# A four-layer network on one core: accumulating scatters, channel mixing in another order, token mixing rewritten

## The reference

```
x = layernorm(x + block_sparse_attention(x))
# mixture of experts 1: E = 8, hidden 512, every token to its 2 best experts, no capacity
probs = softmax(x @ Wg); topv, topi = top_k(probs, 2); topv /= sum(topv)
moe   = sum over the 2 experts of topv * (gelu(x @ Wu[e]) @ Wd[e]);  shared = gelu(x @ W1) @ W2
x = layernorm(x + shared + moe)
# token mixing (a recurrence over the sequence; rms(x) = x * rsqrt(mean(x*x) + 1e-6)), channel mixing
x_in = x; n = rms(x); k, v, r = n @ Wk.T, n @ Wv.T, sigmoid(n @ Wr.T)
state' = ew * state + k*v;  wkv = state + eu * k*v
x = x + mixer_scale * (r * wkv @ Wo.T)
h = leaky_relu(rms(x) @ Wfc.T, 0.5);  x = x + mlp_scale * (h * h @ Wmlp.T)
x = layernorm(x_in + x)          # x_in is what the block was given, x its output
# mixture of experts 2: E = 8, hidden 1024, capacity 640 rows per expert, weights softmax(top 2)
x = layernorm(x + sum over the 2 experts of weight * ((silu(x @ W1[e]) * (x @ W2[e])) @ W3[e]))
```

## Time and profile before

| | us |
|---|---|
| median of 3 runs (2108.09 to 2112.3) | 2112.03 |
| the profiled execution's own time | 2117.18 |
| its span, first to last instruction | 2115.4 |
| PE busy (matmul) | 1739.3 (82%) |
| PE busy (weight load) | 1390.0 (66%) |
| DVE busy | 1202.9 (57%) |
| ACT busy | 881.9 (42%) |
| POOL busy | 599.5 (28%) |
| mean granted TensorE clock | 0.889 of full |

### The profile page before, as it was taken

One profiled execution on the slowest core, in us unless ns is written; L12 is line 12 of the kernel. 1 busy time (PEld: TensorE's weight loads), 2 busy tenths in 40 slices (PEclk: granted clock), 3 DMA queues, 4 the chain that ended last, 5 costly groups with the idle time before them and its releaser, 6 DMA issues. The chain is left out here.

```text
span 2115.4 us, 36910 instructions
## 1 busy us (share of the span) xinstructions
PE 1739.3 (82%) x12492; PEld 1390.0 (66%) x12493; DVE 1202.9 (57%) x2736; ACT 881.9 (42%) x1739; POOL 599.5 (28%) x765
## 2 busy tenths in 40 slices
PE   5759999999994798699999387758887399999970
PEld 4625766666672477577887144457886399999970
DVE  4557677777733766333332488546664655555546
ACT  3200666666682264332232144433442044444336
POOL 1330011111113387423222644122221122312114
PEclk9955899999996599899999699979998599999995
DMA  5694233333303561122222421050001333322206
GB/s 200 245 145 56 53 78 73 76 73 77 75 13 103 172 229 70 50 64 71 64 62 62 142 69 56 0 202 21 21 11 63 100 106 123 108 84 72 77 9 238
DMA packets 142011, 191.00 MB, mean 90 GB/s; under 512 B 70465, under 2 KB 105123, under 8 KB 140864
## 3 DMA queue, kind: packets, MB, share of 16 engines
q1 hardware_dynamic: 113280, 131.79, 20.2%
q0 software_dynamic: 20992, 51.80, 9.0%
q10 hardware_dynamic: 7616, 5.77, 1.5%
HBM read 125.98 MB, written 65.54 MB: 91 GB/s over the span
## 5 line engine op out<-in xcount | busy, mean ns | idle before, releaser
L583 DVE TENSOR_REDUCE att_neg_max<-att_m_ps 128x1 f32<-128x320 f32 x496 | 234.7, 487 | 129.9 <-PE att_m_ps L410 122.3
L410 PE MATMUL att_m_ps<-att_k,att_q 96*128 96x384 f32 x496 | 229.3, 474 | 28.4 <-DMA att_k<-qk 21.0
L1827 PE MATMUL silu_h_ps<-silu_xT,silu_w_part 128*128 128x320 f32 x1536 | 237.9, 312 | 6.4 <-DVE silu_h L1935 3.2
L1827 PEld LDWEIGHTS silu_h_ps<-silu_xT,silu_w_part 128*128 128x128 f32 x1536 | 227.7, 189 | 9.4 <-issue 4.1
L410 PEld LDWEIGHTS att_m_ps<-att_k,att_q 96*128 96x128 f32 x496 | 103.6, 209 | 137.3 <-DVE att_neg_max L583 87.6
L1612 PE MATMUL gelu_y_ps<-layer_wd,gelu_hT 128*128 x576 | 138.0, 382 | 7.8 <-issue 7.1
L548 ACT ACTIVATE att_prob_f<-att_b_ps 128x1024 f32<-128x1024 f32 x64 | 65.6, 1024 | 172.6 <-PE att_b_ps L434 172.6
L2380 PE MATMUL mlp_y_ps<-mlp_wm_part,mlp_h_part 128*128 128x256 f32 x768 | 108.9, 311 | 28.2 <-DVE mlp_h_part L2491 28.2
L2380 PEld LDWEIGHTS mlp_y_ps<-mlp_wm_part,mlp_h_part 128*128 128x128 f32 x768 | 107.3, 220 | 30.4 <-DVE mlp_h_part L2491 30.4
L1573 POOL DMA_INDIRECT gelu_x<-rows,gelu_row_no x72 | 71.7, 996 | 173.7 <-PE gelu_x_ps L1584 156.5
L1612 PEld LDWEIGHTS gelu_y_ps<-layer_wd,gelu_hT 128*128 128x128 f32 x576 | 103.8, 190 | 23.3 <-issue 12.0
(11 more groups left out here) (313 smaller groups left out, 3825.3 us busy)
## 6 DMA issues: line engine op xcount, KB each, us to landing
experts_w<-in_dram SPq DMA_DIRECT2D x24, 1024.0 KB
qk<-qkv_part POOLq DMA_DIRECT2D x32, 512.0 KB, 3.3
att_k<-qk SPq DMA_DIRECT2D x192, 64.0 KB, 2.3
att_q<-qk SPq DMA_DIRECT2D x168, 64.0 KB, 3.0
expert_rows<-gelu_y SPq DMA_DIRECT2D x72, 128.0 KB, 1.7
expert_rows<-mlp_zero SPq DMA_DIRECT2D x8, 1024.0 KB, 16.5
v<-qkv_v POOLq DMA_DIRECT2D x8, 544.0 KB, 4.8
att_v<-v SPq DMA_DIRECT2D x8, 544.0 KB, 4.2
```

The source lines that it names most:

```text
L410: nc.tensor.matmul(bank[:, 0:2 * LOCAL].rearrange("p (a n) -> p a n", a=2), q[b][0:MROW, x, :], local_and_global(b, x), start=True, stop=T ...
L583: ins = nc.vector.tensor_reduce(neg_max[p % 2][:, x:x + 1], m_ps[u % 2][:, 0:LOCAL + 2 * BLK], AX.X, ALU.max, negate=True)
L1827: mm = nc.tensor.matmul(h_ps[u % 2][a][:, :], w12_part[f % RING][wp][:, a, k, :], xT[s][xp][:, k, rows], start=(i == 0), stop=(i == 3 * KD ...
```

## The change

It has five parts.

1. *First experts.* DVE multiplies y by `share`, a weight for each row of each tile, when it takes it from PSUM, and POOL adds the tile to `part` (which holds x + shared) with an accumulating indirect DMA. Each waits for the landing of the one before. The gather of tile n + 6 stands ahead of the scatter of tile n in POOL's queue; y gets four buffers. Empty rows have number T and are skipped. The second experts do the same into `summed`, with five buffers.
2. *Routing.* The one-hot product gives four columns instead of one or two: the token's number and the two halves (high, rest) of its weight, for either choice; `in_tile` gets three columns for each choice. From it come `table` (both forms of the row number) and `share`.
3. *Token mixing.* It reads `part` alone; no gathers and no weighted sums. Both norms' roots come from one variance, the first scaling (n1) moves to ACT, the second rms scaling goes: since leaky relu and square turn a scaling of a row into its square, the factor `share` (one over the mean square) is put on in channel mixing's last addition. The order on all engines is new, with products, turns and projections dealt among one another; base has three buffers.
4. *Channel mixing.* The downs of group g - 1 stand between the ups of group g, after slices 2, 4, 5 and 7, and the turn of group g - 2 before the last slice; `h_part` has two buffers, `out` is written over x. The normed rows are stored twice, to `rows` and to `summed` (the start value of the second experts' sum). No zeros are written.
5. *End and loops.* `combine` becomes `last_norm`: it loads `summed` (4 MB) and does the layer norm, statistics on DVE, scaling on ACT. All hardware loops over groups, tiles and experts are written out.

```diff
@@ experts_gelu
-        @block.sync
-        def _(sp):
-            with sp.Fori(0, NT // 2) as i:
-                for s in range(2):
-                    n = 2 * i + s
-                    sp.wait_ge(y_ready, n + 1)
-                    sp.dma_start(y_d[bass.ds(n * P, P), :], y[s][:, :]).then_inc(y_out[s], 16)
...
+            def gather(n):
+                s = n % XS
+                if n >= XS:
+                    pool.wait_ge(x_turned, n - XS + 1)
+                nc.gpsimd.indirect_dma_start(out=x[s][:, :], out_offset=None, in_=x_d,
+                                             in_offset=bass.IndirectOffsetOnAxis(ap=table[:, 1, n:n + 1], axis=0)
+                                             ).then_inc(x_in[s], 16)
+
+            for n in range(XS + 2):
+                gather(n)
+            for n in range(NT):
+                if n + XS + 2 < NT:
+                    gather(n + XS + 2)
+                pool.wait_ge(y_ready, n + 1)
+                if n > 0:
+                    pool.wait_ge(y_out, 16 * n)
+                nc.gpsimd.indirect_dma_start(out=sum_d, out_offset=bass.IndirectOffsetOnAxis(ap=table[:, 0, n:n + 1], axis=0),
+                                             in_=y[n % YS][:, :], in_offset=None, bounds_check=T - 1, oob_is_err=False,
+                                             compute_op=ALU.add).then_inc(y_out, 16)
...
-                dve.wait_ge(y_out[s], 16 * (n // 2))
-                nc.vector.tensor_copy(y[s][:, :], y_ps[s][:, :]).then_inc(y_ready, 1)
+                if n >= YS:
+                    dve.wait_ge(y_out, 16 * (n - YS + 1))
+                nc.vector.tensor_scalar(y[n % YS][:, :], y_ps[s][:, :], share[:, n:n + 1], None, ALU.mult).then_inc(y_ready, 1)
@@ route
+            settle(nc.vector.tensor_copy(halves[:, :, :], weight[:, :, :]))
+            for a in range(2):
+                nc.vector.tensor_copy(entry[:, :, a, 2 * a], tokens[:, :])
+                nc.vector.tensor_copy(entry[:, :, a, 1 - a], halves[:, a, :].bitcast(F32))
+                settle(nc.vector.tensor_tensor(entry[:, :, a, 2 - a], weight[:, a, :], halves[:, a, :].bitcast(F32), ALU.subtract))
...
-                nc.vector.tensor_tensor(in_tile[half % HALVES][:, :, :, :], in_tile[half % HALVES][:, :, :, :].bitcast(F32),
-                                        tokens[:, bass.ds(N * q, N)].rearrange("p (t a b) -> p t a b", a=1, b=1).broadcast_to(tiled),
+                spread = [P, 2 * N, COLS - 1, NT]
+                nc.vector.tensor_tensor(in_tile[half % HALVES][:, :, :, :, :].rearrange("p t a c n -> p (t a) c n"),
+                                        is_tile[half % HALVES][:, :, :, :].rearrange("p t (a b) n -> p (t a) b n", b=1).broadcast_to(spread),
+                                        entry[:, N * q:N * (q + 1), :, :].rearrange("p t a (c b) -> p (t a) c b", b=1).broadcast_to(spread),
                                         ALU.mult).then_inc(made, 1)
@@ mix_tokens, VectorE's step (all of it is new)
+            def step(g):
+                if exists(g + 2):
+                    stats(g + 2)
+                if exists(g + 1):
+                    scan(g + 1, 0)
+                if exists(g + 2):
+                    inverses(g + 2)
+                if exists(g):
+                    add(g, (0,))
+                if exists(g + 1):
+                    weigh(g + 1, 0)
...
+                if exists(g):
+                    add(g, (2, 3))
+                if exists(g + 2):
+                    normalised(g + 2)
+                if exists(g + 1):
+                    scan(g + 1, 1)
+                    weigh(g + 1, 1)
+                    gated(g + 1, 1)
+                if exists(g - 1):
+                    shares(g - 1)
@@ mix_channels, TensorE
-            def step(g, s):
-                if exists(g):
-                    for f in range(1, KF):
-                        up(g, s, f)
-                if exists(g + 1):
-
-                    up(g + 1, 1 - s, 0)
-                if exists(g - 2):
-                    norm.turn(pe, g - 2, s)
-                if exists(g):
-                    down(g, s)
-
-            skewed(pe, -1, 2, step, start=4)
+            for g in range(NGRP + 3):
+                for f in range(KF):
+                    if exists(g):
+                        up(g, f)
+                    if exists(g - 1) and f in AFTER:
+                        down(g - 1, AFTER.index(f))
+                    if exists(g - 2) and f == KF - 2:
+                        norm.turn(pe, g - 2, g % 2)
@@ mix_channels, VectorE's addition
-                    nc.vector.tensor_tensor(out[s][:, j, :], y_ps[j % 2][:, :],
-                                            x[:, bass.ds(g * GT + j, 1), :].rearrange("p a d -> p (a d)"),
-                                            ALU.add).then_inc(summed, 1)
+                nc.vector.scalar_tensor_tensor(out[g][:, j, :], y_ps[j % 2][:, :], share[:, t:t + 1], x[:, t, :],
+                                               ALU.mult, ALU.add).then_inc(summed, 1)
```

1017 lines of the change are left out of this document (449 added, 568 removed).

## The result

The changed kernel takes **2062.2 us** (median of four runs, 2058.7 to 2067.6) beside 2112.2 for the kernel before on the same chip: a ratio of 0.977, 95% interval 0.974 to 0.979. The forecast was 2027, its range 1996 to 2080. So the sign and the range held, and the gain is 50 us where the sum said 85.

The account below looks back on a forecast made before the run. No single engine bounds the program; gaps lie in the stages rewritten. Terms 0 + 7 + 6 - 49 - 31 - 18 = -85 take the profiled 2117.2 us to 2032, 2027 as median; range 1996 to 2080.

Parts of the forecast that it names:

- the first experts' scatter: First experts: accumulating scatters in one chain would leave the stage's time unchanged, 0 us, with ends of -18 and +142.
- I take 4.0: First experts: assumed scatter cycle of 4.0 us, against a step of 4.02 before.
- L: First experts: the accumulating scatter's cycle, issue to next issue, in us; between 3.24 and 6.05, taken as 4.0.
- rival (2): First experts: the chain costs, but less than is won, cycle 4.5 to 5.2 us, total 2061 to 2110; chance 0.14.
- rival (1): First experts: the chain hides, cycle under 3.76 us, TensorE sets the pace, -18 more, total 2009; chance 0.18.
- give back 1 us: First experts: the last landing at the end costs the 1 us saved by the step, leaving 0.
- Token mixing (-49, measured -60): Token mixing: TensorE becomes the bound, 16.4 us per group for -36, and an earlier start for -13; together -49.
- the best case: Token mixing: the most favourable end of the term, -60 us.
- Channel mixing (-31, measured -36): Channel mixing: the wait for the last split falls away, 24.2 us per group, seven groups save 5.0 each; -31 in all.
- Rival (3): Channel mixing: VectorE becomes the bound, a group stays at 29 us, total 2058; chance 0.07.
- Routing (+13, measured +11.6): Both routings: wider one-hot multiplies on VectorE cost +7 us in the first and +6 in the second.
- last stages (-18, measured -22.8): Second experts and last normalisation: scatters hidden but +1.5 us, half the bytes loaded, additions gone; together -18, from -12 to -22.

Follow-up runs that it names:

- Experiment 1: Changed kernel with the first experts' 72 scatters writing plainly instead of adding, all waits kept: 1996.2 us, ratio 0.944.
- Experiments 6 and 7: Changed kernel with channel mixing's second products all at once after the next group's first product (2134.6 us), or one group behind but undealt (2089.7 us).
- experiment 4: Changed kernel with no bound on the row numbers of the first experts' scatters, empty slots getting rows of their own: 2066.4 us, ratio 0.9756.
- experiment 2: Changed kernel with even tiles of the first experts added into one tensor and odd ones into another, merged on GpSimd: 2012.3 us, ratio 0.951.

## Why the prediction came out as it did

*The step that failed: the first experts' scatter, "I take 4.0".* L is 4.745. The text said that each tenth is 7 us and that the forecast is wrong first of all if L lies outside 3.8 to 4.4. It does: 63 steps x (4.745 - 4.02) = 46 of the +57.7. Of the other 12, 3.6 lie ahead of the first scatter and 8 behind the 64th, where the backlog of scatters is issued. Seen from PE, its last product comes 39 us later in the stage, and the tail behind it is 18 us longer. The mechanism was the one described (one chain, the scatter waiting for its landing), and rival (2) had its number, 4.5 to 5.2. Rival (2) is what happened. That the time still came out well inside the range is luck: the first experts alone would have put the forecast at 2085. Token mixing gave 11 more than forecast, channel mixing 5, the last stages 5 and the routings 1, and so it became 2062.

Why 4.0 was too low, in its own words: "most of an accumulating DMA is the plain one with a second read beside the first". Experiment 1 measures both forms in one place. The issue is not the plain one: 1.57 instead of 1.02, which rival (2) had named as its condition and the sum had not. The landing is 0.7 later behind it. 3.24 plus 0.55 to 0.6 plus 0.7 is 4.5; the median step is 4.67, so about 0.1 of it is not placed. The text's own argument against rival (1), "twice the descriptors", pointed at the first part; it was used against the rival and left out of the sum. That the longer issue comes from the additional packets (96 for each scatter) fits, but was not shown. Rival (1)'s size is settled too: with the chain hidden the stage takes 295 to 298 us, 9 to 12 below before, not 18.

*Where the sum and the tail meet.* I let the stage's end give back 1 us for a last landing. With a chain slower than PE the tail is a backlog: up to four results, then the empty tiles, 22 us from PE's last product to the next stage where it was 4.

*Token mixing (-49, measured -60).* PE is the bound, as forecast. The group is 15.66 and not 16.4: the pieces of my sum overlap at every change of kind (six projections at 1.71, 3.6 for the output products, 1.75 for all turns). The head takes 9.4 us from the first load to the first turn where I took 12 to 13. The stage's gain, 60.2, is what the prediction had called the best case.

```profile
1238.58 1.41 DVE L2113 BATCH_NORM_STATS2 mix_part<-mix_base 128x6 f32<-128x256 f32 x4 [3.08 <-DMA mix_base<-part]
...
1242.60 2.07 ACT L2037 ACTIVATE mix_n<-mix_base,mix_shift,mix_inv 128x256 f32<-128x256 f32 x4 [0.47 <-DVE mix_shift L2123]
...
1244.72 1.97 PE L1959 MATMUL mix_turn_ps<-all_ident,mix_n 128*128 128x128 f32 x8 [31.86 <-ACT mix_n L2037]
```

The load (issued at 1235.28) is used after 3.3 us, not after the 4.5 that I had read in the last stage of the kernel before, which loads 8 MB from its start.

*Channel mixing (-31, measured -36).* Right in its mechanism. The group is PE's own work, 23.40, without the 0.8 of waiting that I had added. The 29.2 of before was also too long: it is one group, read from the start of its first products to the end of its second ones, and six groups have a mean of 28.4. The two errors cancel, so the 5.0 us for each of seven groups came out right by luck. What the dealing gives back is the wait and the granted clock behind it, 0.92 from 1440 to 1610 before and 1.00 from 1440 to 1590 now. Rival (3), VectorE as the bound, didn't come: it is busy 139.7 of 217 us. Experiments 6 and 7 show that both halves of the edit count, and that the dealing protects something I had not named, the turn of the normalised rows.

*Routing (+13, measured +11.6), last stages (-18, measured -22.8).* Right in sign, and near in size; the last stages gave 0.8 more than my best case of -22. From the first routing's own first DMA to the first gather it is 136.1 us before and 141.9 now, 140.9 to 143.4 in the nine experiments that leave this stage as it is. Its multiply takes 1.94 to 3.05 us and most bursts wait for it:

```profile
833.88 3.03 DVE L1432 TENSOR_TENSOR route_in_tile<-route_at_tile,route_entry 128x1728 fp32r<-128x1728 f32 x1
...
836.96 1.15 PE L1140 MATMUL route_table_ps<-route_in_tile,route_in_slot 128*128 128x216 f32 x8 [2.29 <-DVE route_in_tile L1432]
```

The last stage runs on ACT without gaps from the first scaling on, as forecast; the answer for before is the earlier trace rows:

```profile
2045.16 2.08 ACT L984 ACTIVATE combine_out<-combine_x,combine_shift,combine_inv 128x256 f32<-128x256 f32 x4 [0.21 <-DVE combine_shift L958]
...
2058.09 4.02 ACT L984 ACTIVATE combine_out<-combine_x,combine_shift,combine_inv 128x256 f32<-128x256 f32 x8
```

*Still open.* What fills the 0.77 to 0.85 us between the landing that a scatter waits for and its issue: experiment 4 only excludes the bound. Why issuing the accumulating form takes 0.55 us more. Why the kernel before takes 10 us longer on one chip than on another: its only trace is from the first.

## What to carry to other kernels

A chain of accumulating DMAs is priced by its own cycle, wake-up, issue, both passes over memory and landing, and compared with the pace of the loop before anything else; here 4.7 us against 3.8 cost 67 us, more than any other term gained. Such a chain is split, not buffered: two destinations took its waiting out of the step here, while more buffers only changed which engine the profile names. A scatter that replaces a gather moves its cost into the producer's loop, so look whether that loop has the slack.

## What the runs showed that I had not expected

- The accumulating scatter of 128 rows of 1 KB is issued in 1.57 us where the plain one takes 1.02 or less, and lands 3.8 us after its start instead of 2.5. In experiment 2 the next scatter, to the other tensor, is issued just as the one before lands (0.03 us ahead of it in the median), so whether two in flight slow each other is not shown.
- Halving the rows takes 0.5 us from the landing and nothing from the issue.
- A scatter whose rows are all out of bounds still costs 3.5 us in the chain.
- The waits of 2 to 5 us in channel mixing cost twice: the granted clock is 0.50 to 0.53 in the 3 or so us behind them, and 1.00 throughout where PE has no wait.
- An order that is tolerable in one version of a stage can be worse in another: nearly the same order of products gives groups of 28.4 us in the old channel mixing and of about 33 in the new.
